# The three scale operations of the next unit, moved behind the first three chunks of the recurrence over chunks

## The reference

```
proj  = layernorm(x) @ W_in.T                     # gate, value_raw, step parameters of 32 heads
value = silu(causal conv of 4 taps(value_raw))
bc    = value @ W_bc.T  -> (row, t, head, 4, 32)
bc    = bc / (sqrt(sum(bc*bc, over the 32)) + 1e-8)      # Bz, Bx, Cz, Cx
for t in time:                                           # a damped oscillator for each state
    S = 1 / (1 + dt*k + dt*dt*A)
    z = S * (z - dt*A*s + dt*(Bz x u))
    s = s + dt*z + dt*(Bx x u)
    y = Cz . z + Cx . s
out = ((y + skip*value) * silu(gate)) @ W_out.T
```

## Time and profile before

| | |
|---|---|
| median of 3 runs | 2289.22 us (2287.39 to 2293.16) |
| the profiled execution: its own time | 2283.27 us |
| its span | 2281.6 us |
| TensorE matmuls busy | 1919.5 us (84%) |
| TensorE weight loads busy | 1069.0 us (47%) |
| VectorE busy | 1873.0 us (82%) |
| ScalarE busy | 1397.6 us (61%) |
| GpSimd busy | 85.5 us (4%) |

### The profile page before, as it was taken

The page is one execution under the profiler, slowest core; times in us unless marked ns, Lnnn a source line. Parts: engine busy times, 40 slices in busy tenths (PEclk is TensorE's granted clock), DMA queues, the critical chain, the costliest instruction groups (busy, mean ns, idle before and its releaser), DMA issues. The chain is left out here.

```text
span 2281.6 us, 79802 instructions
## 1 busy us (share of the span) xinstructions
PE 1919.5 (84%) x31786; PEld 1069.0 (47%) x31786; DVE 1873.0 (82%) x5468; ACT 1397.6 (61%) x1829; POOL 85.5 (4%) x28
## 2 busy tenths in 40 slices
PE   6787428999999999999999998999999998358886
PEld 3343204554455445444544444444544454347675
DVE  6788438998889899889989898898889987486764
ACT  4666335776677677667767776676767656035453
POOL 0000000000000000000000000000000000153300
PEclk9889668999999999999999999999999999578997
DMA  4554622233333333333333342343334221533400
GB/s 140 187 184 171 189 60 72 86 108 93 90 91 107 83 106 104 86 88 97 111 83 90 91 119 81 86 116 85 95 89 112 71 65 48 193 135 115 148 28 28
DMA packets 165405, 235.85 MB, mean 103 GB/s; under 512 B 60048, under 2 KB 86672, under 8 KB 158864
## 3 DMA queue, kind: packets, MB, share of 16 engines
q1 hardware_dynamic: 115152, 147.61, 21.0%
q10 hardware_dynamic: 48704, 78.68, 11.9%
q0 software_dynamic: 1152, 4.19, 0.6%
HBM read 175.84 MB, written 51.39 MB: 100 GB/s over the span
## 5 line engine op out<-in xcount | busy, mean ns | idle before, releaser
L668 PE MATMUL m_ps_a<-m_valT,m_w_bc 128*128 128x512 f32 x2048 | 957.0, 610 | 59.1 <-ACT m_raw L854 40.5
L668 PEld LDWEIGHTS m_ps_a<-m_valT,m_w_bc 128*128 128x128 f32 x2048 | 373.2, 193 | 499.4 <-issue 486.0
L992 DVE TENSOR_TENSOR m_prod<-m_psi,m_shear 128x128 f32<-128x128 f32 x960 | 274.9, 286 | 0.0
L997 DVE TENSOR_TENSOR m_psi<-m_psi,m_prod 128x128 f32<-128x128 f32 x960 | 270.6, 282 | 0.0
L853 ACT ACTIVATE m_sq<-m_ps_a 128x512 f32<-128x512 f32 x256 | 154.0, 602 | 185.9 <-PE m_ps_a L668 181.4
L842 ACT ACTIVATE m_psi_g<-m_psi 128x2080 f32<-128x2080 f32 x64 | 245.8, 3840 | 0.0
L702 PE MATMUL m_ps_g<-m_q,m_k 32*64 32x64 f32 x8192 | 123.6, 235 | 53.2 <-issue 40.0
L702 PEld LDWEIGHTS m_ps_g<-m_q,m_k 32*64 32x64 f32 x8192 | 108.3, 136 | 107.5 <-ACT m_dX L875 61.2
L854 ACT ACTIVATE m_raw<-m_ps_a 128x512 f32<-128x512 f32 x256 | 151.0, 590 | 0.0
L875 ACT ACTIVATE m_dX<-m_ps_g 128x128 f32<-128x128 f32 (+1 forms) x128 | 26.8, 261 | 197.2 <-PE m_ps_g L711 170.8
L222 PE MATMUL ps_w<-p_xnT,w_in 128*128 128x512 f32 x256 | 119.2, 620 | 18.3 <-ACT gate L285 18.3
(11 more groups left out here) (153 smaller groups left out, 3321.4 us busy)
## 6 DMA issues: line engine op xcount, KB each, us to landing
m_w_bc<-in_w_bcT ACTq DMA_DIRECT2D x252, 256.0 KB, 2.8
m_stage<-scratch_shear SPq DMA_DIRECT2D x240, 128.0 KB
m_det<-scratch_gd SPq DMA_DIRECT2D x256, 64.0 KB, 2.1
scratch_gateT<-gate SPq DMA_DIRECT2D x8, 1024.0 KB, 3.9
scratch_valT<-val SPq DMA_DIRECT2D x8, 1024.0 KB, 4.5
scratch_svgT<-svg SPq DMA_DIRECT2D x8, 1024.0 KB, 5.7
scratch_u<-p_u SPq DMA_DIRECT2D x8, 1024.0 KB, 7.7
m_valT<-scratch_valT SPq DMA_DIRECT2D x32, 256.0 KB, 5.1
```

The source lines that it names most:

```text
L668: mm = pe.matmul(ps_a[j % 2].ap(), w_bc[:, j, kt, :], valT[:, kt, :], start=(kt == 0), stop=(kt == KI - 1), skip_group_check=True)
L992: dve.tensor_tensor(prod.ap().rearrange("p r k c -> p r (k c)"), psi[:, half, t].rearrange("p r k c -> p r (k c)"), shear[:, half, t].rear ...
L997: ins = dve.tensor_tensor(psi[:, half, t + 1], psi[:, half, t], prod[:, :, ::-1, :], ALU.add)
```

## The change

The helper that did all three scale operations becomes three helpers. Their place moves from in front of the recurrence over chunks into it: the first operation behind chunk 0, the second behind chunk 1, the third behind chunk 2. The `advance(1)` that stood behind each of the three is gone, so that three psi steps of the unit stay for the end of its share. The waits of the three are the same, at the new places. In the prologue (unit 0's scales) the three are called one after another, as before.

```
-                def scales(b, group, between):
-
+                def add_eps(b, group):
                     dve.wait_ge(compact_in.sem, compact_in.at(b, (group + 1) * NJ - 1))
                     dve.tensor_scalar(compact.ap(), compact.ap(), NORM_EPS, None, ALU.add).then_inc(own.sem, own.one())
-                    between(1)
-                    dve.wait_ge(own.sem, own.n)
+                    return own.n
+
+                def invert_norms(eps_added):
+                    dve.wait_ge(own.sem, eps_added)
                     dve.reciprocal(compact.ap(), compact.ap()).then_inc(own.sem, own.one())
-                    between(1)
+                    return own.n
+
+                def apply_factors(b, group, inverted):
                     dve.wait_ge(factor_in.sem, factor_in.at(b, 3 * (group + 1) - 1))
-                    dve.wait_ge(own.sem, own.n)
+                    dve.wait_ge(own.sem, inverted)
                     dve.tensor_tensor(compact.ap(), compact.ap(), factor.ap(), ALU.mult).then_inc(rows_ready.sem, rows_ready.step)
-                    between(1)
...
-                        scales(0, 0, lambda n: None)
+                        apply_factors(0, 0, invert_norms(add_eps(0, 0)))
...
+                        here = not (last and group == LAST)
...
-                        if not (last and group == LAST):
-                            scales(b, group + 1, advance)
...
                             dve.tensor_tensor(X[:, c], flat[:, 0:4:3], flat[:, 1:3], ALU.subtract).then_inc(X_ready.sem, X_ready.step)
                             advance(1)
+                            if here and c == 0:
+                                eps_added = add_eps(b, group + 1)
+                            if here and c == 1:
+                                inverted = invert_norms(eps_added)
+                            if here and c == 2:
+                                apply_factors(b, group + 1, inverted)
```

## The result

On the chip of the first comparison the changed kernel took 2300.24 us (median of 5 runs, 2299.13 to 2304.3), the kernel before 2290.99 us (5 runs, 2287.39 to 2293.16): ratio 1.0046, interval 1.0033 to 1.0059, 9.3 us slower. On a second chip, where both were run again beside the experiments, it was 2321.57 us (6 runs) against 2303.53 us (23 runs): ratio 1.0083, interval 1.0061 to 1.0106, 18 us slower. The forecast was 19 us: half of it came on the first chip, nearly all of it on the second.

A forecast was written before the change was run, and what follows sets the result against it. PE's queue was taken to set a unit's length, with DVE following in waits. Terms 9 + 9 + 1 = 19 us on the profiled 2283.3 gave 2302; the runs' median, 5.9 us above, made it 2308 us, range 2290 to 2322.

The forecast's parts named there:

- What bounds the kernel: All units: PE's own queue sets a unit's length, DVE follows with waits; gain in front of the recurrence 0.
- The place of the chain: DVE's recurrence: the third scale operation ends 3.44 us after its start, 4.16 us later than before in unit 21.
- Units without the pause: About 9 units without PE's pause within the scores, group 1 apart: scale rows 1.0 us late at the broadcast, 9 us.
- Units with the pause: About 46 units where PE pauses within the scores: half in time, rows 0.2 us late on average, 9 us.
- Group 1: 8 units where the norms come last: broadcast at 597.64 against 597.47 in unit 9, taken as 0.1 each, 1 us.
- still in time: Unit 21: masked scores 0.71 us later, so the broadcast could go at 899.92, before its start at 899.98.
- slack that the change may spend: Unit 21 before the change: scale rows land 3.5 us ahead of PE's broadcast, which the change spends.
- What was moved off the wait at the end: Unit's end on DVE: three psi steps at 0.28 us each in place of 0.20, costing PE nothing in units 21 to 24.
- The clock: Rival: new PE waits of 1.0 us slow the clock in 9 units, 15 us more, 2323; 0.09 with chain above 5.2 us.

The follow-up runs named there:

- only the signal late: Kernel before with the scale operations at their old place; only the signal to SP that the scale rows are ready given behind chunk 2: 1.0063.
- norms first: Kernel before with SP's loads of the compact norms in group 1 issued ahead of the next shear's load: 2283.16 us, 0.9908.

## Why the prediction was right, and where its steps were not

**What bounds the kernel: right.** PE's queue sets the unit; DVE's gain in front of the recurrence turned into waits for dX (47.3 to 112.9 us). DVE is nearer to the bound than I had it: 0.7 us more of it a unit and PE waits for keys in 20 units.

**The place of the chain: right.** The third operation was put 3.44 us behind the start of the recurrence and ended after 3.33. The wait moved from the masks to the transfer of the rows, longest in group 5, as forecast.

**Units without the pause (group 5): 1.0 forecast, 1.45 to 1.6 found**, and the step hides two errors. Compared with the run that has only the signal late, the store leaves 0.85 us later (3.44 against 2.59 after dX) and the loads land 1.25 us later (3.82 against 2.57); 0.48 us was to spare: 1.62, against 8.90 - 7.25 = 1.65 from dX to the broadcast. So without the collision with the load of the weights the rows would be 0.4 us late, and with it 1.6. I had missed the collision and counted 0.3 us from landing to broadcast, where it takes 0.04.

**Units with the pause: 0.2 forecast, about nothing found.** Groups 2, 3, 4, 6 and 7 sum to +0.56 us over the five on the first chip and -0.53 on the second. On the first chip the store lands sooner than in the earlier trace rows, the loads in 2.5 to 2.9 us, and on average the rows are 0.2 to 0.9 us ahead of the broadcast in groups 0, 2, 3, 4, 6 and 7. The store's landing in the changed kernel:

```profile
DMA to landing us min/median/max: 1.5/1.5/2.8
```

By the sentence on the Trainium skill's fixed cost of 2.0 us ("DMA: Bandwidth & Descriptors", Anatomy of one DMA — SWDGE (gpsimd) path) for both, the sum was to be 35 us. That section is on transfers that GpSimd issues, which the prediction did not say; these are SyncE's. The store took less, and 9 to 18 us were measured.

**Group 1: 0.1 forecast, 0.7 to 1.0 found, by another mechanism.** The step that I worked out, norms, chain, broadcast, came out as said: 9.20 us from dX to the broadcast, 9.22 before. The step that failed stands one unit earlier: the masks 0.71 us later, "still in time", and 3.5 us ahead of PE as slack that the change may spend. In group 0 the masks came 0.58 us later and the rows 5.7 us, and both are in time for the broadcast. But PE's queue goes on from them to the jump, which takes some 5 us and was just hidden; the prediction has no term for it.

**What was moved off the wait at the end: right.** The psi steps cost nothing that can be told (1.0005). **The clock: it did not fall.** 0.98 over the units in both kernels; the broadcast of unit 21 took 1.14 us right after its wait of 1.57.

**Not forecast:** units of group 0 are 0.8 to 0.9 us shorter. The pauses before their outputs L756 went from 1.56 to 0.93 us a unit, those before the chunk states L711 from 0.64 to 1.11, and the product matmuls took 0.3 us less. I have no cause for it.

By units, group 5 gives 8 x 1.60 = 12.8 us on the first chip, group 1 8 x 0.70 = 5.6, groups 2 to 4 8 x 0.31 = 2.5, groups 6 and 7 7 x 0.25 = 1.8, and group 0 takes back 7 x 0.83 = 5.8: 16.9 of the 17.5 us between the profiled executions. That the forecast sum of 19 us is near this is luck: it had 9 us for the units without the pause, 9 for those with it and 1 for group 1, and found are 12.8 us (group 5), -1.5 (groups 0, 2 to 4, 6 and 7) and 5.6. On the second chip the same sum is 8.9 of the 11.3 us between the traces; its medians differ by 18, and the traces do not show the rest. Open stays too why the change costs 28 us by the medians on top of norms first: its profiled execution is the fastest of its 12 runs, and the traces account for 14 (2300.79 against 2286.92).

## What to carry to other kernels

Slack in front of an instruction may be in use though the instruction never waits: an in-order queue that passes its waits early can do what stands behind them, here a jump of nearly 5 us that was hidden only because the queue came to it early. So ask what a queue does with the time before spending it, and look for the instructions that the timeline leaves out. Before a transfer is moved to a later place, look for the large transfers that are issued at that place by other engines. And look for the wait of a transfer queue that holds up something small: the best version here came from the order of SP's loads, not from the operations.

## What the runs showed of the hardware

**Pauses marked "issue" on PE follow packets of its program.** In the kernel before, 50 pauses of over 0.3 us before the scores L702 (400 to 1900 us) end 1.20 to 1.64 us after the end of a 16 KB packet of q8, those before L756 and L711 1.23 to 1.52 us. In unit 22 the scores stop and go on

```profile
916.36 0.68 PE L702 MATMUL m_ps_g<-m_q,m_k 32*64 32x64 f32 x36
918.36 1.31 PE L702 MATMUL m_ps_g<-m_q,m_k 32*64 32x64 f32 x92 [1.32 <-issue]
```

and between 915.3 and 916.9 us the transfers of that queue are

```profile
q8 instruction: 1, 0.02, 5.5%
```

one packet, which took 1.41 us (5.5% of 16 engines in 1.6 us). So PE, with four such packets a unit, seems to be short of program in the runs of small matmuls; the four lines "issue" of PE with more than a microsecond in all are 74 us of 1500 (39.8, 17.3, 12.5 and 4.4). The Trainium skill ("Runtime: NRT & Kernel Launch", Instruction fetch mechanics) says that crossing such a block is mostly hidden; here the trace differs.

**A jump back to the start of a loop held PE's queue** for 3.5 to 5.8 us (84 jumps in 14 traces), one that was not taken for 0.08 us (14). PE meanwhile worked off the matmuls that stood ahead of it.

**A load of 256 KB beside four of 8 KB:** in group 5 the four landed 3.8 us after the first issue with the change, 2.8 us with one large load moved away, and 2.6 us where only the signal was late.
